# A graph-attention edge stream on one Trainium2 core: the next block's exponent chain begins at the tenth addition, its steps spread over the pairs

## The reference, cut to what matters

```python
feats = jnp.einsum('nf,hfo->hno', x, W)             # 4 heads, 64 columns each
z = s_self[:, edge_row] + s_neigh[:, edge_col]
e = jnp.where(z > 0, z, LEAKY_ALPHA * z) * adj_val[None, :]
def seg_softmax(e_h):
    m = jax.ops.segment_max(e_h, edge_row, num_segments=N)
    ex = jnp.exp(e_h - m[edge_row])
    s = jax.ops.segment_sum(ex, edge_row, num_segments=N)
    return ex / s[edge_row]
def aggregate(alpha_h, feat_h):
    return jax.ops.segment_sum(alpha_h[:, None] * feat_h[edge_col], edge_row, num_segments=N)
```

## Time and profile before

| what | us |
|---|---|
| median of three timed runs | 2572.36 |
| span of the profiled execution | 2885.5 |
| the edge stream in it, first pair matmul to the end of its additions | 1278.2 |
| one block of 32 pairs there, 25 starts of line 1038 | 50.3 |
| block 24, the last with a chain, start of its first pair matmul to that of block 25 | 34.4 |

### The profile page before, as it was taken

The page is one execution under the profiler, slowest core; times in us unless marked ns, Lnnn a source line. Parts: engine busy times, 40 slices in busy tenths (PEclk is TensorE's granted clock), DMA queues, the critical chain, the costliest instruction groups (busy, mean ns, idle before and its releaser), DMA issues. The chain is left out here.

```text
span 2885.5 us, 41185 instructions
## 1 busy us (share of the span) xinstructions
PE 1974.6 (68%) x8208; PEld 1382.7 (48%) x8209; DVE 1712.1 (59%) x3913; ACT 1407.0 (49%) x4790; POOL 1307.5 (45%) x1293
## 2 busy tenths in 40 slices
PE   4888866755246666665665666666757369999966
PEld 2555543432123333343343434343446369999954
DVE  6988798988135454544545445455678234444458
ACT  2544443332246747566565765747754124434434
POOL 2322200001735656656665565656217546666622
PEclk9999985556655656666666665657765579999987
DMA  4000000000423433333343333334153823333345
GB/s 151 21 19 19 19 6 0 0 0 10 122 85 102 112 96 108 109 106 106 102 112 99 103 110 105 108 98 112 36 176 42 115 68 106 107 101 106 104 134 165
DMA packets 133144, 245.18 MB, mean 85 GB/s; under 512 B 32277, under 2 KB 81347, under 8 KB 133009
## 3 DMA queue, kind: packets, MB, share of 16 engines
q0 software_dynamic: 54176, 140.57, 18.0%
q1 hardware_dynamic: 70190, 94.19, 11.1%
q10 hardware_dynamic: 8642, 9.08, 1.8%
HBM read 208.85 MB, written 34.88 MB: 84 GB/s over the span
## 5 line engine op out<-in xcount | busy, mean ns | idle before, releaser
L1019 POOL DMA_INDIRECT big<-feat_d,pair_idx x832 | 798.9, 960 | 552.3 <-PE wide L1144 294.1
L1144 PE MATMUL wide<-big 128*128 128x260 f32 x1664 | 757.0, 591 | 171.0 <-ACT big L1046 105.6
L1046 ACT ACTIVATE big<-big 128x64 f32<-128x64 f32 x3328 | 803.9, 336 | 16.1 <-issue 14.7
L1391 DVE TENSOR_TENSOR big<-big,wide 128x260 f32 x832 | 352.9, 424 | 580.4 <-PE wide L1144 340.0
L1144 PEld LDWEIGHTS wide<-big 128*128 128x128 f32 x1664 | 389.1, 275 | 298.9 <-ACT big L1046 186.3
L1108 PEld LDWEIGHTS wide<-score_parts,hot_t 128*128 128x128 bf16 x832 | 107.2, 129 | 347.0 <-issue 308.8
L1108 PE MATMUL wide<-score_parts,hot_t 128*128 x832 | 110.5, 188 | 199.8 <-DVE hot_t L1304 88.4
L1038 ACT ACTIVATE wide<-wide 128x4 f32<-128x4 f32 x26 | 4.1, 158 | 475.1 <-PE wide L1135 458.5
L2007 PEld LDWEIGHTS p_h<-xT,w_sb 128*128 128x128 f32 x1808 | 221.2, 193 | 8.0 <-issue 2.3
L2007 PE MATMUL p_h<-xT,w_sb 128*128 128x128 f32 x1808 | 221.7, 276 | 2.0 <-issue 2.0
L311 ACT ACTIVATE big<-big 128x896 f32<-128x896 f32 (+2 forms) x153 | 137.7, 900 | 169.9 <-DVE big L595 152.5
(11 more groups left out here) (347 smaller groups left out, 3184.7 us busy)
## 6 DMA issues: line engine op xcount, KB each, us to landing
big<-code_d SPq DMA_DIRECT2D x52, 512.0 KB
big<-in_L_ffn_w_dram SPq DMA_DIRECT2D x32, 512.0 KB
b_sb<-in_L_ffn_b_dram SPq DMA_DIRECT2D x113, 128.0 KB
big<-feat_d,pair_idx POOLq DMA_INDIRECT x832
big<-moe_d SPq DMA_DIRECT2D x7, 1792.0 KB, 9.9
feat_d<-feat_sb SPq DMA_DIRECT2D x49, 130.0 KB, 2.1
y_d<-Y ACTq DMA_DIRECT2D x7, 896.0 KB
X<-in_x_dram SPq DMA_DIRECT2D x6, 1024.0 KB, 11.9
```

The costliest lines, as they stand in the source:

```text
L1019: nc.gpsimd.indirect_dma_start(out=rows[:, n // SB % RB, n % SB, :], out_offset=None, in_=m["feat_d"], in_offset=bass.IndirectOffsetOnAxis ...
L1046: ins = nc.scalar.activation(rows[:, b, s, cols], rows[:, b, s, cols], ACT.Copy, scale=rows[:, b, s, HF + h:HF + h + 1])
L1144: nc.tensor.matmul(sums[s % RING][:, 0:HF + H], onehot[:, s // GP % 2, s % GP, :], rows[:, b, s, :], start=True, stop=True).then_inc(summe ...
L1391: nc.vector.tensor_tensor(of, of, sums[s % RING][:, 0:HF + H], ALU.add).then_inc(added, 1)
```

## The change

On DVE the chain's pieces move to earlier additions, on PE its four turns with them, on ACT `head` moves from pair 12 to pair 4. `sum_self` of the block after moves from a block's start to its 25th addition, and the second `turn_hot` from the end to addition 28. The first operand of a small matmul in `turn_arg` becomes a tile of its own, `first_hot`, made by one more DVE instruction in `heads`.

```diff
             def step(k, b, turn):                    # ACT
                 act.wait_ge(ex_made, 2 * k + 2)
-                scale(k, b, range(0, 6))
-                scale(k, b, range(6, 12))
+                scale(k, b, range(0, 4))
                 if there(k + 1):
                     head(k + 1)
-                scale(k, b, range(12, SB))
+                scale(k, b, range(4, SB))
...
             def turn_arg(k):                         # PE
                 pe.wait_ge(drop_made, k + 1)
-                pe.wait_ge(hot_made, k * (SB // GP) + 1)
                 wait_turn(pe, ex_made, 2 * k)
-                nc.tensor.matmul(p_arg[:, HS:HS + H], onehot[0:1, 0, 0, :], drop[:], start=True, stop=True)
+                nc.tensor.matmul(p_arg[:, HS:HS + H], first_hot[:], drop[:], start=True, stop=True)
...
+                    if s == 12:
+                        turn_z(k + 1)
+                    elif s == 17:
+                        turn_ends(k + 1)
+                    elif s == 21:
+                        turn_carry(k + 1)
+                    elif s == 25:
+                        turn_arg(k + 1)
...
             def heads(k):                            # DVE
+                wait_turn(dve, arg_turned, k)
+                nc.vector.tensor_tensor(first_hot[:], lane[0:1, :], pair_rel[0:1, ds(k * SB, 1)].to_broadcast([1, P]), ALU.is_equal)
...
             def step(k, b, turn):                    # DVE
-                if more:
-                    sum_self(k + 1)
                 fade_row(k, tile)
-                add(k, tile, range(0, 8))
+                add(k, tile, range(0, 3))
+                if more:
+                    heads(k + 1)
+                add(k, tile, range(3, 8))
                 select(k, 2)
-                add(k, tile, range(8, 11))
+                add(k, tile, range(8, 10))
+                if more:
+                    scores(k + 1, 1 - b, turn + b)
+                add(k, tile, range(10, 11))
                 if later:
                     turn_hot(2 * k + 5)
-                add(k, tile, range(11, 16))
-                select(k, 3)
-                if more:
-                    heads(k + 1)
-                add(k, tile, range(16, 22))
-                if more:
-                    scores(k + 1, 1 - b, turn + b)
-                add(k, tile, range(22, 24))
+                add(k, tile, range(11, 14))
                 if more:
                     local_max(k + 1)
-                    select(k + 1, 0)
-                add(k, tile, range(24, 26))
+                add(k, tile, range(14, 16))
+                select(k, 3)
+                add(k, tile, range(16, 18))
                 if more:
                     carries(k + 1)
-                add(k, tile, range(26, 27))
+                add(k, tile, range(18, 23))
                 if more:
                     arguments(k + 1)
-                add(k, tile, range(27, SB))
+                add(k, tile, range(23, 25))
+                if more:
+                    select(k + 1, 0)
+                if later:
+                    sum_self(k + 2)
+                add(k, tile, range(25, 28))
+                if there(k + 3):
+                    turn_hot(2 * k + 6)
+                add(k, tile, range(28, SB))
                 if more:
                     select(k + 1, 1)
-                if there(k + 3):
-                    turn_hot(2 * k + 6)
```

More of the change, by code:

```diff
@@ L878, in edge_stream @@
     drop = sb("drop", [1, H])
+    first_hot = sb("first_hot", [1, P])
     wide = [ps(f"wide{i}", [P, 1024]) for i in range(4)]
@@ L1130, in turn_arg, with add_up @@
                 pe.wait_ge(drop_made, k + 1)
[L1131 removed]
                 wait_turn(pe, ex_made, 2 * k)
[L1133 removed]
+                nc.tensor.matmul(p_arg[:, HS:HS + H], first_hot[:], drop[:], start=True, stop=True)
                 wait_apart(pe, arg_made, k + 1, crossed)
                 nc.tensor.transpose(p_arg[:, 0:HS], arg[:], ident[:]).then_inc(arg_turned, 1)
[L1137 to L1147 removed]
+            def add_up(k, b, s):
+                n = k * SB + s
+                if s % GP == 0:
+                    pe.wait_ge(hot_made, k * (SB // GP) + (s // GP + 1))
+                pe.wait_ge(scaled, n + 1)
+                pe.wait_ge(added, n + 1)
+                nc.tensor.matmul(sums[s % RING][:, 0:HF + H], onehot[:, s // GP % 2, s % GP, :], rows[:, b, s, :],
+                                 start=True, stop=True).then_inc(summed, 1)
@@ L1149, in step @@
             def step(k, b, turn):
                 more, later = there(k + 1), there(k + 2)
-                for half in range(2):
-                    lo = half * HB
-                    if later:
+                for s in range(SB):
+                    half, at = s // HB, s % HB
+                    if later and at == 0:
                         tile = tiles_of(mybir.EngineType.PE, (2 * k + (4 + half)) * (HB // PACK), HB // PACK)
-                        add_up(k, b, range(lo, lo + 8), lambda s: look_up(k + 2, half, tile, (2 * (s - lo), 2 * (s - lo) + 1)))
-                    else:
-                        add_up(k, b, range(lo, lo + 8))
-                    if half == 0:
-                        add_up(k, b, range(8, HB))
@@ L1160, in step @@
-                if more:
-                    turn_z(k + 1)
-                add_up(k, b, range(24, 26))
-                if more:
-                    turn_ends(k + 1)
-                add_up(k, b, range(26, 27))
-                if more:
-                    turn_carry(k + 1)
-                add_up(k, b, range(27, 28))
-                if more:
-                    turn_arg(k + 1)
-                add_up(k, b, range(28, SB))
+                    add_up(k, b, s)
+                    if later and at < HB // 2:
+                        look_up(k + 2, half, tile, (2 * at, 2 * at + 1))
@@ L1173, in first @@
+                    if not more:
+                        continue
+                    if s == 12:
[6 more added lines that the diff above has]
+                        turn_arg(k + 1)
             def first(k):
@@ L1441, in _ @@
             turn_hot(4)
+            sum_self(1)
             dve.wait_ge(zeroed, 1)
```

15 lines of the change are left out of this document (1 added, 14 removed).

## The result

The change makes the kernel slower: 2580.93 us (median of 8 runs, 2579.0 to 2587.43) against 2572.02 us (8 runs, 2563.06 to 2577.11) for the kernel before, a ratio of 1.0039 with a 95% interval of 1.0027 to 1.0051. That is a loss of 0.4%: small, but clear of the noise. The forecast of 2550 us was wrong in sign; the third rival, "slower", had named +9 us and 2581.

What follows compares the result with a forecast made beforehand. DVE was taken to bound each edge-stream block, and gathers after the change: 1.4 + 960 + 3 + 50 = 1014 us against 1033, -19, or -35 with quicker gathers; forecast -22, 2572 - 22 = 2550 us, range 2480 to 2583.

Steps and rivals of the forecast that it cites:

- third rival: Edge stream, "slower": gathers already set the pace, more work follows the last ones; +9 us, 2581 us; chance 0.20.
- Who carries a block without gathers: Edge-stream block: DVE carries it, in its chain as well as in its additions; block 24 takes 34.4 us.
- Block 24's sum of 39.0 us: Ordinary block without pauses: block 24's 34.4 plus 1.4 one-hots, 1.0 tile-number loads and 2.2 PE's late start.
- The pauses and their share: Edge stream: most pauses are a burden of recording; 245 of 313 us fall there, leaving 1033 us timed.
- The savings on DVE, -3.1 us a block: DVE's block: -1.7 end waits, -1.9 late start, +0.2 comparison, +0.3 PE waits; 40.5 to 37.4 us.
- New waits on PE, 0.3 us a block: PE's turns amid pairs hold later pairs until DVE makes their input; bounds 0 and 1.0 us, 0.3 taken.
- What is late next: Edge stream after the change: gathers at 1.25 us set the pace; 1.4 + 960 + 3 + 50 = 1014 against 1033.
- my floor for before, 1006 us: Edge stream before, if gathers already set the pace: 1.4 + 960 + 3 + 41.4 = 1006 us at least.
- The work behind the last gather: End of edge stream: 3 us landing, then 41.4 us plus 12 additions and a select, less 1.7: about 50.
- No gather limit: Edge stream: POOL issues in 1.15 us or less unrecorded, DVE's saving comes in full; -75 us, about 2495; chance 0.25.
- The pauses are real: Edge stream: timed blocks also take 50.3 us, and 3.1 us or more each go; -75 to -100 us; chance 0.12.
- What would show it: Trace signs: gathers 1.25 us apart, DVE idle before scores, PE's sum_self wait gone, ACT's 17 us wait a remnant.

Runs made afterwards that it cites:

- e5: Kernel before with every other gather of blocks 2 to 25 left out; 2549.84 us, ratio 0.9912 to the kernel before.
- e15: Kernel before with the one-hot made by a two-operand comparison, its second operand read from PSUM; 2618.98 us, ratio 1.0169.
- the second trace: Kernel before, unchanged, profiled again; 2576.84 us, ratio 1.0013 to itself; that profiled execution took 2568.45 us with a span of 2566.7.
- e6: Changed kernel with every other gather of blocks 2 to 25 left out; 2459.39 us, ratio 0.956 to the kernel before.
- e3: Changed kernel with the chain begun later in every block, scores after addition 15, PE turns behind pairs 18, 22, 25, 29; 2581.93 us, ratio 1.0029.
- e9: Changed kernel once more, nothing altered, on another chip; 2584.86 us, ratio 1.0047 to the kernel before.
- e4: Changed kernel with the chain at its old place (scores after addition 21) in every block, seam changes kept; 2580.13 us, ratio 1.0017.

## Why the prediction was wrong

- **Who carries a block without gathers: right.** Block 24's sum of 39.0 us was measured as 39.5 (e5), and e15 shows that it is DVE's. In the last block it is not: after its exponents ACT scales for 31.1 us without a pause.
- **The pauses and their share: right.** I gave the edge stream 245 of 313 us, 1033 us in all. Against the second trace, the stream is 1278.2 - 1036.1 = 242.1 us longer in the first; 58.0 came ahead of it (first exponents at 819.1 and 761.1), and 777.7 - 758.7 = 19.0 behind it. The pauses were not a burden of recording, though: no later profiled execution has them, and spans lie 1.7 us below the time. So the block of 46 to 47 us and the span of about 2800 that I forecast for the profile of the changed kernel did not come either (41.1 and 2577.9). What made the pauses is open. The rule of the Trainium skill that I had set against my reading ("Runtime: NRT & Kernel Launch", "The ~15µs preamble/postamble breakdown": about 6 us between profile and execution time) is nearer to these 1.7 us than to 313, though there the profile is the longer of the two and here the execution is; I had called it contradicted, from a trace whose own execution time was not recorded.
- **The savings on DVE, -3.1 us a block: right in kind, a little small.** -3.5 by 25 blocks of e5 and e6.
- **New waits on PE, 0.3 us a block: not as put.** PE waits 148.5 us in 24 turns of `z`, some 6.2 us each, since it stands there as long as `scores` waits for rows (waits of PE, changed kernel):

```profile
PE wide L1117 <- issue: 148.5, 24, 11.5
PE wide L1142 <- DVE big L1385: 115.1, 120, 4.5
```

  It costs nothing while the gathers are the pace, and with half of them it is 36.5 us in 24.
- **What is late next: here it failed.** That gathers of 1.25 us set the pace of the changed kernel was right. The sum "1.4 + 960 + 3 + 50 = 1014 us" was not: its terms measure 20.4 + 975.5 + 53.5 = 1049.4. The first, 1.4 us, is the worst, 19.0 us too small. I let the 65th gather wait for the first sum; but the first gather starts at 706.1, 64 of them take 83.3 us, and when the first pair matmul runs (769.0), POOL still has 20.4 us to go. In the first trace the first pair matmul came only at 829.6, and the 64 gathers were done by then. The second, 960, is 15.5 us too small: the pitch is 1.27 us for 1.25, with the gathers that DVE holds. The same two errors sit in my floor for before, 1006 us: it measures 20.2 + 969.1 + 46.8 = 1036.1. With the first term right in both, the floor of before would have been 1025 and that of after 1033, beside an estimate of 1033 for before, and there was no room for -19 us. The comparison set an estimate from observed times on one side (1033) against a floor on the other (1014); the difference of the two floors, +8 to +9, had the right sign all along.
- **The work behind the last gather: the number right, the reason not.** 3 + 50 = 53 was measured as 4.3 + 49.2 = 53.5, but I had priced it as 12 more additions at 0.78 us and a `select`. It is the chain's spread (+5.6 us) and ACT's block behind it; by additions e3 would have given back 4.7 us, and it gave 1.4. That the term came out is luck.
- **The rivals.** "No gather limit": refuted, no gather in any trace is shorter than 0.94 us or has less than 0.30 us ahead of it, with or without pauses. "The pauses are real": refuted. "Slower", with its deciding point (POOL's block longer than DVE's before the change): 40.4 against 39.5, it held. Its price, more work behind the last gathers, was forecast as +8.6 and measured as +6.7 us in the tail; the longer gather run, +6.2, it did not have. The timed loss is 8.9 us here, 13 by the traces, so that its 2581 is the measured median to 0.1 us is in part luck.
- **What would show it.** Gathers 1.25 us apart and DVE idle before `scores`: seen. PE's wait for `sum_self` at the block's start is gone (83.6 us in the second trace of before, none among the changed kernel's waits). ACT's wait did not fall to a remnant as I had said (210.9 to 222.4 us over 24): ACT has 31.1 us of work in a block of 41, and the rest stays slack.

## What to carry to other kernels

Write the length of a stream as one formula (start of the pacing engine's work, its steps, the tail behind the last) and fill it in for before and after alike; never set an observed time against a floor. In a loop paced by a producer, ask what stands behind the producer's last item: steps of a dependent chain that were spread out to fill gaps lengthen it by their spread, so keep the last round's steps close together if need be. An instruction that costs its own engine nothing can still hold another engine's without any semaphore between them; look at the producer's own durations before and after. Look at a second profiled execution when span and timed median differ by more than a few us.

## What the runs showed of the hardware that was not expected

- A bf16 comparison of 128 x 2048 from SBUF to SBUF with a scalar column holds a GpSimd gather that runs beside it: 0.2 to 0.4 us on average for the 0.75 us form (7.4 us over 47 gathers in e9, 16.9 over 39 in e4), 3.9 us on average (the one shown lasted 5.04 us instead of 0.95) for the strided form. The two-operand form with its second operand read from PSUM takes 2.28 us and holds none.
- The strided form takes 4.77 us for the same elements, 6.4 times the plain one.
- Gathers over 1.0 us long also occur beside small DVE instructions (0.27 us each in `heads`): 34 gathers lose 5.3 us beside `heads`, the scans and `carries` in the changed kernel. That these instructions hold them is read from the overlap in time; no run removes them.
- One execution of the kernel before had 319 us of pauses (span 2885.5 against 2566.7) that no other profiled execution of it or its variants shows.
